# Moving the dense products of a three-layer gated graph network ahead in the order, and its last tiles ahead of them

## The chip, the cores and the metric

The kernel runs on one core of one Trainium2 chip. The metric is the device time of one execution in microseconds, as the median of several runs.

## What is computed

`x` has 12500 rows of 128 numbers, and there are 212500 edges `src -> dst`, sorted by `dst`. The reference normalises `x`, applies a ReLU and a linear layer, then runs three layers of message passing with a gated recurrent cell, and adds the result to `x`:

```python
h = jnp.maximum(_layernorm(x, axis=-1), 0.0)
h = h @ lin_w.T + lin_b
for i in range(3):
    m = h @ weight[i]
    agg = jax.ops.segment_sum(m[src], dst, num_segments=n_nodes)
    h = gru_cell(agg, h, w_ih, w_hh, b_ih, b_hh)
return x + h
```

A layer needs the messages `m` of all nodes of the layer before, since an edge may come from anywhere.

## The kernel before

Edges stand in 416 quads of 512 edges, and 28 quads make a superblock, of which there are 15. The sums `agg` are made in two ways. Of each superblock, 16 quads are **dense**: in the first part of layer one (the text counts layers from one, the code from zero) the kernel counts on the chip how often each source row feeds each destination, stores these counts as bytes, and from then on a dense quad's sum is a product of message rows and counts. The other 12 quads are **gathered**: POOL issues one indirect DMA for each 128 edges (line 600) into a ring of four steps' rows (`RING`), and PE adds them with one-hot matrices (line 880).

The program of each layer is a list of *steps*, the same for all engines. Step s of a layer handles two gathered quads: eight gathers on POOL, 24 matmuls on PE, two additions into `aggT` on DVE (line 1290). POOL may be four steps ahead of PE. Layer one has 144 steps, of which the last 46 (98 to 143) have dense work; layers two and three have 88 steps each. After a layer's last numbered step come a few more without gathers.

Dense work is counted in *units* of two or three blocks of 128 source rows; 42 units make one superblock's dense sum, 14 slices of three units. For one unit ACT widens the counts from bytes (`widen`, line 717), DVE splits the message rows into two halves (`split`, lines 1404 and 1406), and PE does two matmuls per block (`dense_block`, line 920). `wide_counts` and `message_halves` have two slices each (`UBUF`), so ACT and DVE can be six units ahead of PE. In every step with dense work PE takes `STEP_UNITS`, that is seven, units. When a superblock's 42 units are done, DVE adds its sum to `aggT` (line 1301).

A *tile* is 256 destination nodes, 49 of them. A tile's work begins in the first step after its quads have been added (`ready_after`, `schedule`): three products of the state (lines 838 to 840) and three of the sums (line 868) on PE, sigmoids on ACT (662, 665), then DVE and a tanh (672), the new state (1344). In the step after the next come the next layer's messages on PE (851), which ACT copies (690, 692) and which leave as three bf16 pieces in one store (706, `store`). In the last layer line 849 transposes the result and line 709 stores it. Where `gates_last` holds, a tile's products stand at the end of a step, after the units; otherwise ahead of them.

The layers join at one wait: POOL gathers nothing of layer n+1 until every message store of layer n has landed (`pool.wait_ge(s_mst, 16 * NT * layer)`, ahead of line 600). Up to 30 units of the next layer may be done ahead, because their message rows come from tiles that are long done (`dense_blocks(True)`, limited by `TAIL_SPARE`). The order on each engine is written out at build time by `layer_steps`; `dense_blocks` says which blocks belong to which step, `units_and_sums` puts a widen and a split six units ahead of their product.

## Time and profile before

| what | value |
|---|---|
| median of three runs | 3803.09 us (3802.09 to 3811.09) |
| the profiled execution's own time | 3803.88 us |
| its span, first to last instruction | 3802.1 us |
| busy share of the span | PE 88%, DVE 74%, ACT 80%, POOL 70% |
| chain that ended last, by engine | POOL 35%, PE 23%, issue 15%, ACT 15%, DVE 6%, DMA 4% |
| granted TensorE clock, mean | 0.96 of full speed |

The span has six stretches: the prologue and the counting up to about 1316 us; the dense steps of layer one, whose last gathered sum on PE begins at 1797.61 us; a passage in which the last tiles are finished, up to layer two's first gather at 1885.95 us; layer two, whose last gathered sum begins at 2812.16 us; a second passage, up to 2859.75 us; and layer three to the end. A view by stretches reads better here than the page's sums, because the engine that sets the pace changes. In a timeline row the columns are start in us, duration in us, engine, line, operation, output<-inputs, count, and in brackets the idle time ahead of the first instruction with what ended it. Rows of a timeline that follow each other on one engine and line are merged.

### The profile page before, as it was taken

To read this page: it belongs to the slowest core of one execution; us is meant where nothing else is said; L and a number is where in the kernel's file an instruction comes from. 1 tells how busy PE (TensorE), PEld (TensorE's weight loads), DVE (VectorE), ACT (ScalarE), POOL (GpSimd) and SP (SyncE) were. 2 spreads that over 40 slices of the span, in tenths; PEclk is the share of its full clock that TensorE was granted. 3 is DMA by queue.
4 is the path that set the end of the run, shared out by engine and by line. 5 is a ranking of instruction groups with operands and counts; after the bars stand their busy time and mean duration, and the time that the engine had idled before them with its cause. 6 is when DMAs were issued, how large, how long until landed. Compare 5 with 4: busy or idle time off the path is not lost.

```text
span 3802.1 us, 76920 instructions
## 1 busy us (share of the span) xinstructions
PE 3361.6 (88%) x24880; PEld 2652.7 (70%) x24881; DVE 2801.6 (74%) x7778; ACT 3044.4 (80%) x4427; POOL 2663.4 (70%) x2622
## 2 busy tenths in 40 slices
PE   5279888998999799999799999999987999999997
PEld 4156666666666577777577777777776877787775
DVE  7678787888887677777577777777775777777775
ACT  4268898888888788888788889888886888878784
POOL 4677776776766677775177777777736777777775
PEclk8589999999999899999899999999998999999999
DMA  8345545455554697776666777777775766666674
GB/s 273 112 120 191 175 156 181 148 184 166 164 184 145 194 275 213 212 212 187 196 199 201 219 207 217 218 207 214 210 226 180 207 203 202 205 201 205 200 210 126
DMA packets 445139, 736.12 MB, mean 194 GB/s; under 512 B 63688, under 2 KB 329032, under 8 KB 444744
## 3 DMA queue, kind: packets, MB, share of 16 engines
q1 hardware_dynamic: 206616, 402.21, 32.7%
q0 software_dynamic: 122880, 251.82, 24.5%
q10 hardware_dynamic: 115248, 77.10, 6.5%
q8 instruction: 213, 3.49, 0.4%
q14 instruction: 182, 1.49, 0.1%
HBM read 557.22 MB, written 173.67 MB: 192 GB/s over the span
## 4 chain that ended last, share of the span: by engine, by line
POOL 35%; PE 23%; issue 15%; ACT 15%; DVE 6%; DMA 4%; ACTq 1%; DVEq 0%; SPq 0%; POOLq 0%
POOL ring_region L600 34%; PE psum L903 16%; ACT wide_counts L717 10%; ACT half_counts L758 3%; DMA states<-temps 2%; DVE quad_onehots L1370 2%; PE psum L920 2%; PE psum L880 1%; PE psum L868 1%; DVE block_onehots L1354 1%; PE psum L811 1%; DVE temps L1330 1%; DMA messages_region<-counts 1%; PE psum L804 0%; ACTq L745 0%
## 5 line engine op out<-in xcount | busy, mean ns | idle before, releaser
L600 POOL DMA_INDIRECT ring_region<-messages,edge_src x2560 | 2609.2, 1019 | 1037.5 <-issue 764.2
L717 ACT CAST wide_counts<-messages_region 128x1024 fp32r<-128x1024 uint8 (+1 forms) x1596 | 1762.0, 1185 | 188.5 <-PE psum L920 155.1
L920 PE MATMUL psum<-wide_counts,message_halves 128*128 128x512 f32 x7448 | 1794.4, 398 | 70.3 <-DVE message_halves L1406 50.5
L920 PEld LDWEIGHTS psum<-wide_counts,message_halves 128*128 128x128 f32 x7448 | 1397.6, 191 | 374.8 <-ACT wide_counts L717 90.0
L903 PE MATMUL psum<-quad_onehots,block_onehots 128*128 128x266 bf16 (+1 forms) x6720 | 844.7, 272 | 104.2 <-ACT half_counts L758 63.8
L758 ACT CAST half_counts<-psum 128x490 f32 (+1 forms) x1680 | 846.9, 594 | 64.6 <-PE psum L903 40.2
L903 PEld LDWEIGHTS psum<-quad_onehots,block_onehots 128*128 128x128 bf16 x6720 | 576.4, 100 | 359.5 <-issue 137.0
L1406 DVE TENSOR_TENSOR message_halves<-messages_region,message_halves 128x256 fp32r<-128x256 f32 (+1 forms) x1596 | 751.0, 471 | 55.0
L1404 DVE CAST message_halves<-messages_region 128x256 fp32r<-128x256 f32 (+1 forms) x1596 | 611.4, 383 | 114.1 <-PE psum L920 75.7
L1370 DVE TENSOR_SCALAR quad_onehots<-iota_quad,count_keys 128x1176 bf16<-128x1176 f16 x960 | 560.7, 645 | 0.0
L880 PE MATMUL psum<-onehot,ring_region 128*128 128x36 bf16 x7680 | 245.0, 179 | 151.7 <-DMA ring_region<-messages,edge_src 140.8
L880 PEld LDWEIGHTS psum<-onehot,ring_region 128*128 128x128 bf16 x7680 | 230.8, 97 | 210.6 <-issue 180.0
L1354 DVE TENSOR_SCALAR block_onehots<-iota_block,count_keys 128x128 bf16<-128x128 bf16 x960 | 183.6, 271 | 137.9 <-PE psum L896 101.4
L1290 DVE TENSOR_TENSOR aggT<-aggT,psum 128x36 f32 x640 | 122.2, 191 | 216.4 <-PE psum L880 147.8
L1330 DVE SCALAR_TENSOR_TENSOR temps<-psum,small,temps 128x256 f32<-128x256 f32 x147 | 70.8, 482 | 241.3 <-ACT temps L662 236.4
L868 PE MATMUL psum<-aggT,wih 128*128 128x256 f32 x882 | 217.1, 383 | 3.7 <-DVE aggT L1301 3.7
L868 PEld LDWEIGHTS psum<-aggT,wih 128*128 128x128 f32 x882 | 169.8, 193 | 27.7 <-issue 4.1
L662 ACT ACTIVATE temps<-psum,small 128x256 f32<-128x256 f32 x147 | 69.0, 469 | 142.9 <-PE psum L868 142.7
L672 ACT ACTIVATE temps<-temps,small 128x256 f32<-128x256 f32 x147 | 76.2, 518 | 106.1 <-DVE temps L1332 105.9
L1265 DVE TENSOR_TENSOR onehot<-iota_block,edge_rel 128x288 bf16<-128x288 bf16 x320 | 144.7, 452 | 1.5 <-issue 1.5
L700 ACT CAST pieces_out<-temps 128x256 bf16<-128x256 f32 x98 | 41.9, 427 | 121.9 <-DVE temps L1309 121.9
L762 ACT CAST half_counts<-psum 128x98 f32 x210 | 128.1, 610 | 0.0
(132 smaller groups left out, 1788.4 us busy)
## 6 DMA issues: line engine op xcount, KB each, us to landing
messages_region<-counts SPq DMA_DIRECT2D x532, 462.0 KB
counts<-half_counts SPq DMA_DIRECT2D x210, 462.0 KB
ring_region<-messages,edge_src POOLq DMA_INDIRECT x2560
messages<-pieces_out ACTq DMA_DIRECT2D x98, 192.0 KB
messages_region<-plain SPq DMA_DIRECT2D x21, 896.0 KB, 8.0
temps<-states ACTq DMA_DIRECT2D x98, 128.0 KB
states<-temps ACTq DMA_DIRECT2D x98, 128.0 KB
plain<-temps ACTq DMA_DIRECT2D x98, 128.0 KB
```

Of the source, the lines that this page charges most:

```text
L600: nc.gpsimd.indirect_dma_start(out=rows[:, n % RING, h * QC + c, :], out_offset=None, in_=messages[layer], in_offset=bass.IndirectOffsetOn ...
L717: nc.scalar.copy(wide_counts[:, v % UBUF, here], stage[v % ABUF][:, here, :, 0:WW]).then_inc(s_wide, 1)
L758: nc.scalar.copy(half_counts[half][:, 2 * HB * i:2 * HB * (i + 1), own:WS][:, :, bass.ds(columns[j], W - own)], counted[:, 0:RW].rearrange ...
L868: nc.tensor.matmul(bank, wih[:, gate * P:(gate + 1) * P], nodes, start=alone, stop=True, skip_group_check=not alone).then_inc(s_gate, 1)
L880: mm = nc.tensor.matmul(window(n, h), rows[:, n % RING, i, k * P:(k + 1) * P], onehot[:, n % 3, i, :], start=(c == 0 and k == 0), stop=(c ...
L903: mm = nc.tensor.matmul(by_block[:, :, SUBLOW[c]:SUBLOW[c] + SUBW[c]], blocks_oh[j % 3][:, c, :], x_round, start=(k == 0), stop=True, skip ...
L920: mm = nc.tensor.matmul(psum[:, 6 + kg % 2, 0:2 * WW], halves[:, v % UBUF, b % HB, half * P:(half + 1) * P], wide_counts[:, v % UBUF, b % ...
L1265: nc.vector.tensor_tensor(onehot[:, n % 3, :, :], iota_lo[:, 0:W].unsqueeze(1).to_broadcast([P, 2 * QC, W]), edge_rel[:, first * QC:(first ...
L1354: made = nc.vector.tensor_scalar(blocks_oh[j % 3][:, c, :], iota_lo[:], los[:, col:col + 1], None, ALU.is_equal)
L1370: made = nc.vector.tensor_scalar(xs[j % 2][c], iota_x[:, 0:NB * SUBW[c]], keys[:, col:col + 1], -float(SUBLOW[c]), ALU.subtract, ALU.is_equal)
L1404: nc.vector.tensor_copy(high, whole).then_inc(s_high, 1)
L1406: nc.vector.tensor_tensor(low, whole, high.bitcast(F32), ALU.subtract).then_inc(s_low, 1)
```

## The change

Four things are altered. A step of layer one takes 7.5 units (7 and 8 in turn), a step of the other layers 7.25 (8 in every fourth). Tiles become due by the new pace, exactly counted, in place of a fixed lead of four steps. From the step before a layer's end on, a step has few units (3, then 3, 2 and the rest, `TAIL_UNITS`) and its tile comes first. And from the layer's end on a tile's store stands ahead of the step's widening on ACT.

```diff
-LEAD = 4
+TAIL_UNITS = (3, 3, 2, 20)
...
+    def units_to(layer, i):
+        return (2 * STEP_UNITS + 1) * i // 2 if layer == 0 else (4 * STEP_UNITS + 1) * i // 4
...
-        dense = begun + GSB - 1 - (LEAD if layer else 0)
+        lead = sum(TAIL_UNITS) if layer else 0
+        dense = DENSE_FROM[layer] + next(m for m in range(STEPS[layer])
+                                         if lead + units_to(layer, m + 1) >= UN * SLICES * (i + 1))
...
+        def step_units(layer, s):
+            if not ahead:
+                return STEP_UNITS
+            tail = (STEPS[layer] - 1, *(max(TILES_AT[layer]) + k for k in range(3)))
+            if layer < LAYERS - 1 and s >= tail[0]:
+                return TAIL_UNITS[tail.index(s)] if s in tail else TAIL_UNITS[0]
+            i = s - DENSE_FROM[layer]
+            return units_to(layer, i + 1) - units_to(layer, i)
...
-                now = end if whole else min(block_of(unit_of(d) + STEP_UNITS), max(d, end))
+                now = end if whole else min(block_of(unit_of(d) + step_units(layer, s)), max(d, end))
...
         def gates_last(layer, s):
-            return DENSE_FROM[layer] <= s < STEPS[layer]
+            return DENSE_FROM[layer] <= s < STEPS[layer] - 1
...
+                stores = [low_tile(layer, tiles_at, s, lag) for lag in (3, 2)
+                          if low_tile(layer, tiles_at, s, lag) is not None]
+                if s >= STEPS[layer]:
+                    for t in stores:
+                        store(layer, t)
                 for w in units.get((layer, s), ()):
                     widen(w)
-                for lag in (3, 2):
-                    if low_tile(layer, tiles_at, s, lag) is not None:
-                        store(layer, low_tile(layer, tiles_at, s, lag))
+                if s < STEPS[layer]:
+                    for t in stores:
+                        store(layer, t)
```

Worked out from the tables, the four last tiles and the units around them stand as follows; the number of units in all is the same, 366 up to the end of layer one, 600 for layer two with 30 of them done in layer one and 30 of layer three's done in layer two.

| | before | after |
|---|---|---|
| layer one: units before the sum of its last gathered step (143) | 315 | 337 |
| layer one: steps of its last four tiles | 146 to 149 | 143 to 146 |
| layer one: units after that sum, before the last store / behind it | 51 / 0 | 14 / 15 |
| layer two: units before the sum of its last gathered step (87) | 609 | 630 |
| layer two: steps of its last four tiles | 86, 87, 88, 89 | 84, 85, 86, 88 |
| layer two: units after that sum | 21 | 0 |
| layer three: steps of its last four tiles | 86, 87, 88, 89 | 84, 85, 86, 88 |

PE at the end of layer one, from the products of the last tile (48) to layer two's first gathered sum. 838 to 840 and 868 are a tile's products, 920 the dense matmuls, 851 the messages of the tiles 47 and 48, 880 the gathered sum; the changed file has all PE lines 20 higher. Before:

```order
L838 MATMUL psum<-temps,whh 128x256
L839 MATMUL psum<-temps,whh 128x256
L840 MATMUL psum<-temps,whh 128x256
L868 MATMUL psum<-aggT,wih 128x256 x3
L920 MATMUL psum<-wide_counts,message_halves 128x512 x32
L851 MATMUL psum<-wmsg,temps 128x128 x2
L920 MATMUL psum<-wide_counts,message_halves 128x512 x10
L851 MATMUL psum<-wmsg,temps 128x128 x2
L880 MATMUL psum<-onehot,ring_region 128x36 x24
```

With the change:

```order
L858 MATMUL psum<-temps,whh 128x256
L859 MATMUL psum<-temps,whh 128x256
L860 MATMUL psum<-temps,whh 128x256
L888 MATMUL psum<-aggT,wih 128x256 x3
L940 MATMUL psum<-wide_counts,message_halves 128x512 x14
L871 MATMUL psum<-wmsg,temps 128x128 x2
L940 MATMUL psum<-wide_counts,message_halves 128x512 x10
L871 MATMUL psum<-wmsg,temps 128x128 x2
L940 MATMUL psum<-wide_counts,message_halves 128x512 x70
L900 MATMUL psum<-onehot,ring_region 128x36 x24
```

Between the last tile's products and its messages there are 24 dense matmuls in place of 42, and 70, that is 15 units, now stand behind the messages.

ACT at the same place, from the last tile's tanh (672) on: 690, 692 and 700 are the copies of a tile's messages, 706 its store, 717 the widening; the changed file has these lines 15 higher. Before:

```order
L672 ACTIVATE temps<-temps,small 128x256
L674 ACTIVATE aggT<-ident 128x256
L687 DMA states<-temps 128x256
L690 COPY temps<-psum 128x256
L692 CAST pieces_out<-psum 128x2x128
L694 DMA plain<-temps 128x2x128
L700 CAST pieces_out<-temps 128x2x128
L717 CAST wide_counts<-messages_region 128x1024
L717 CAST wide_counts<-messages_region 128x1536
L706 DMA messages<-pieces_out 128x2x384
```

With the change:

```order
L687 ACTIVATE temps<-temps,small 128x256
L689 ACTIVATE aggT<-ident 128x256
L702 DMA states<-temps 128x256
L705 COPY temps<-psum 128x256
L707 CAST pieces_out<-psum 128x2x128
L709 DMA plain<-temps 128x2x128
L715 CAST pieces_out<-temps 128x2x128
L721 DMA messages<-pieces_out 128x2x384
L732 CAST wide_counts<-messages_region 128x1024
L732 CAST wide_counts<-messages_region 128x1536
```

The store of tile 47 leaves ahead of the two widenings of its step.

PE at the end of layer two, from its last gathered sum to layer three's first. Before, the first ten rows of it:

```order
L880 MATMUL psum<-onehot,ring_region 128x36 x24
L920 MATMUL psum<-wide_counts,message_halves 128x512 x32
L838 MATMUL psum<-third_state_tile,whh 128x256
L839 MATMUL psum<-third_state_tile,whh 128x256
L840 MATMUL psum<-third_state_tile,whh 128x256
L868 MATMUL psum<-aggT,wih 128x256 x3
L851 MATMUL psum<-wmsg,temps 128x128 x2
L838 MATMUL psum<-temps,whh 128x256
L839 MATMUL psum<-temps,whh 128x256
L840 MATMUL psum<-temps,whh 128x256
```

With the change, all of it:

```order
L900 MATMUL psum<-onehot,ring_region 128x36 x24
L871 MATMUL psum<-wmsg,temps 128x128 x4
L858 MATMUL psum<-temps,whh 128x256
L859 MATMUL psum<-temps,whh 128x256
L860 MATMUL psum<-temps,whh 128x256
L888 MATMUL psum<-aggT,wih 128x256 x3
L871 MATMUL psum<-wmsg,temps 128x128 x2
L900 MATMUL psum<-onehot,ring_region 128x36 x24
```

One tile and no unit is left behind the sum, where three tiles and 21 units stood.

## Rows read from the trace of the kernel before

**Rows 1.** POOL's gathers: grouped by line in layer two; the first nine alone (duration min/median/max).

```profile
L600 POOL DMA_INDIRECT ring_region<-messages,edge_src x704 | 703.2, 999 | 327.0 <-issue 213.9 <-DMA messages<-pieces_out 112.7 <-PE psum L880 0.3
...
L600 POOL DMA_INDIRECT ring_region<-messages,edge_src x9: 942/946/949, 1885.9 to 1895.9; - x9
```

**Rows 2.** Timeline of POOL: last gather of layers one and two, first of the next.

```profile
1772.18 1.03 POOL L600 DMA_INDIRECT ring_region<-messages,edge_src  x1 [0.30 <-issue]
...
1885.95 0.94 POOL L600 DMA_INDIRECT ring_region<-messages,edge_src  x1 [112.74 <-DMA messages<-pieces_out]
...
2802.32 1.03 POOL L600 DMA_INDIRECT ring_region<-messages,edge_src  x1 [0.30 <-issue]
2859.75 0.95 POOL L600 DMA_INDIRECT ring_region<-messages,edge_src  x1 [56.40 <-DMA messages<-pieces_out]
```

**Rows 3.** Groups of PE by line: layer two, 1898 to 2812; layer three, 2872 to 3776.

```profile
L920 PE MATMUL psum<-wide_counts,message_halves 128*128 128x512 f32 x2842 | 683.7, 397 | 26.9 <-DVE message_halves L1406 26.9
...
L880 PE MATMUL psum<-onehot,ring_region 128*128 128x36 bf16 x2075 | 66.2, 179 | 20.1 <-DMA ring_region<-messages,edge_src 20.0
...
L880 PE MATMUL psum<-onehot,ring_region 128*128 128x36 bf16 x2077 | 66.4, 179 | 54.9 <-DMA ring_region<-messages,edge_src 54.6
```

**Rows 4.** Timeline of PE, end of layer one: last gathered sum, last tile, next sum.

```profile
1797.61 0.76 PE L880 MATMUL psum<-onehot,ring_region 128*128 128x36 bf16 x24
...
1862.68 1.46 PE L868 MATMUL psum<-aggT,wih 128*128 128x256 f32 x6
...
1897.44 0.88 PE L880 MATMUL psum<-onehot,ring_region 128*128 128x36 bf16 x24 [17.65 <-DMA ring_region<-messages,edge_src]
```

**Rows 5.** Timeline of PE, end of layer two: last gathered sum, last tile, next sum.

```profile
2812.16 0.75 PE L880 MATMUL psum<-onehot,ring_region 128*128 128x36 bf16 x24 [2.02 <-DMA ring_region<-messages,edge_src]
...
2835.82 1.46 PE L868 MATMUL psum<-aggT,wih 128*128 128x256 f32 x6
...
2871.27 0.88 PE L880 MATMUL psum<-onehot,ring_region 128*128 128x36 bf16 x24 [17.87 <-DMA ring_region<-messages,edge_src]
```

**Rows 6.** The page's costliest groups: widening on ACT, the two halves on DVE.

```profile
L717 ACT CAST wide_counts<-messages_region 128x1024 fp32r<-128x1024 uint8 (+1 forms) x1596 | 1762.0, 1185 | 188.5 <-PE psum L920 155.1
...
L1406 DVE TENSOR_TENSOR message_halves<-messages_region,message_halves 128x256 fp32r<-128x256 f32 (+1 forms) x1596 | 751.0, 471 | 55.0
L1404 DVE CAST message_halves<-messages_region 128x256 fp32r<-128x256 f32 (+1 forms) x1596 | 611.4, 383 | 114.1 <-PE psum L920 75.7
```

**Rows 7.** Timeline of PE: gathered sums around a step with a tile and one without.

```profile
1764.99 0.77 PE L880 MATMUL psum<-onehot,ring_region 128*128 128x36 bf16 x24
...
1775.57 0.76 PE L880 MATMUL psum<-onehot,ring_region 128*128 128x36 bf16 x24
...
2790.30 0.77 PE L880 MATMUL psum<-onehot,ring_region 128*128 128x36 bf16 x24
...
2798.28 0.77 PE L880 MATMUL psum<-onehot,ring_region 128*128 128x36 bf16 x24
```

**Rows 8.** Timeline of ACT, end of layer one: a wait for a store, the last store.

```profile
1867.15 0.37 ACT L692 CAST pieces_out<-psum 128x256 bf16<-128x256 f32 x1 [2.60 <-DMA messages<-pieces_out]
...
1883.23 0.37 ACTq L706 DMA_DIRECT2D messages<-pieces_out  x1
```

**Rows 9.** Timelines of PE, end of layer three: last gathered sum, tiles 46, 47, 48.

```profile
3775.80 0.88 PE L880 MATMUL psum<-onehot,ring_region 128*128 128x36 bf16 x24 [7.80 <-DMA ring_region<-messages,edge_src]
3776.52 1.20 PE L838 MATMUL psum<-temps,whh 128*128 128x256 f32 x2
...
3782.29 0.67 PE L838 MATMUL psum<-temps,whh 128*128 128x256 f32 x2 [1.03 <-ACT temps L665]
...
3786.54 0.67 PE L838 MATMUL psum<-third_state_tile,whh 128*128 128x256 f32 x2 [1.21 <-ACT temps L665]
```

**Rows 10.** Timeline of ACT, end of layer two: a wait for a store, the last store.

```profile
2839.01 0.37 ACT L692 CAST pieces_out<-psum 128x256 bf16<-128x256 f32 x1 [2.11 <-DMA messages<-pieces_out]
...
2856.79 0.43 ACTq L706 DMA_DIRECT2D messages<-pieces_out  x1
```

More of the change, by code:

```diff
@@ L119, in gated_graph_layers @@
     STEP_UNITS = UN * SLICES // GSB
-    assert STEP_UNITS * GSB == UN * SLICES and STEP_UNITS <= UBUF * UN + 1
+    assert STEP_UNITS * GSB == UN * SLICES
+    def units_to(layer, i):
+        return (2 * STEP_UNITS + 1) * i // 2 if layer == 0 else (4 * STEP_UNITS + 1) * i // 4
     def block_of(unit):
```

## The prediction

> **What bounds the kernel now.** I read the busy shares first: PE is busiest, POOL least. They mislead, because the pace changes hands between stretches. So I went on to the groups of instructions by line inside each stretch, and then to the timelines of the two passages between layers.
>
> In layer two POOL waits for almost nothing: its gathers show 213.9 us of "issue", a fixed pause of some 0.30 us after each, and 0.3 us of waiting for PE [rows 1]. From the first gather of the layer, 1885.95, to the end of the last, 2802.32 + 1.03, it needs 917.4 us for 88 steps, 10.42 a step [rows 2]. PE meanwhile waits 20.0 us for rows in layer two and 54.6 in layer three [rows 3]. **Inside the layers two and three POOL sets the pace, and PE has a little room.** In layer one's dense part it is the other way: POOL's last gather starts at 1772.18, PE adds that step's rows only at 1797.61 [rows 2, 4]. There PE, fed by ACT and DVE, sets the pace.
>
> **The passages are the loss.** POOL stands idle for 112.74 us and for 56.40 us, each time until the last message store has landed [rows 2]. From the last gathered sum on PE to the next layer's first gather it takes 1885.95 - 1797.61 = 88.3 us, and 2859.75 - 2812.16 = 47.6 us [rows 2, 4, 5]. In them PE works on units of which seven stand around each of the last tiles; after the last store nothing is left for it, and it idles 17.65 and 17.87 us until the new rows come [rows 4, 5]. The change moves units out of the passages: in layer one ahead and behind, in layer two ahead only.
>
> **Prices.** A unit has 14/3 dense matmuls; 2842 of them keep PE busy 683.7 us [rows 3], so a unit costs PE 4.667 x 0.2406 = 1.12 us. ACT widens one in 1762.0 / 1596 = 1.10 us, and DVE splits one in 0.47 + 0.38 = 0.85 us [rows 6]. A step of seven units and a tile takes 1775.57 - 1764.99 = 10.58 us, one without a tile 2798.28 - 2790.30 = 7.98, so a tile costs PE 2.6 us [rows 7].
>
> **Term A, end of layer one.** 337 units instead of 315 now stand ahead of the last gathered sum: 22 x 1.12 = 24.7 us, and two tiles' messages more, 0.9. As PE sets the pace there, the sum comes 25.6 us later. Behind it: the sum and tile 45's products, 0.7 + 2.6 = 3.3 us. Then three more tiles, each with three units on PE: 3.4 + 2.6 = 6.0 us; ACT has three widenings (3.3) and a tile's seven short operations, so I take 6.5 and get 19.5. From tile 48's last product to the last store it is now 1883.23 - (1862.68 + 1.46) = 19.1 us [rows 4, 8]; nine widenings lie in it on ACT, five will, so 19.1 - 4 x 1.10 = 14.7. From the store to the first gather it is 2.7 us [rows 2, 8]. Together 40 in place of 88.3. Gain: 88.3 - 40 - 25.6 = **22.7 us**. The 15 units behind the store take PE 16.8 us. About 2.5 of that passes before the store leaves and 2.7 while it lands, so PE is ready some 12 to 13.5 us after the first gather, where the rows now need 1897.44 - 1885.95 = 11.5: the bubble is filled, at a cost of up to 2 us. Bounds: if the tail's cycles stay at 10.5 us, 12 less; if each of the 22 units costs what a unit costs with all of a step's waits (7 units in 10.58 us: 1.5), 8 less; the other way, tails as short as PE allows and no loss behind, 6 more.
>
> **Term B, layer two.** Now 973.8 us from its first gather to layer three's. PE has more to do before the last sum, 21 units and two tiles: 23.5 + 5.2 us. Against that stand 20.0 us of waiting for rows and 2.02 at the end [rows 3, 5], which go first. So the last sum comes 13.5 + (2812.16 - 1897.44) + 28.7 - 22 = 935 us after the first gather; some of the waits now are followed by slow matmuls, so I take 931. POOL alone would allow 917.4 + 1.8 = 919, PE without any of the room 957; these are the ends. Then the chain: the sum (0.7); tile 47's state, for which I take the 4.25 us from one tile to the next without units, 3782.29 to 3786.54 [rows 9]; tile 48's products, 2.6. From there to the last store it is now 2856.79 - (2835.82 + 1.46) = 19.5 us with seven widenings in it [rows 5, 10], without them 11.8; and 3.0 us to the gather. That makes 22 in place of 47.6. Layer two then takes 931 + 22 = 953: gain **20.8 us**. Nothing is left to fill this passage, but PE's idling there costs nothing that POOL does not cost anyway.
>
> **Term C, layer three.** PE has 54.6 us of room [rows 3] for 21 units ahead, so POOL's pace stands: the last sum comes, as now, 3775.80 - 2859.75 = 916 us after the first gather. Now 26.3 us follow with three tiles; then one. From tile 48's first product to the end it is 3802.1 - 3786.54 = 15.6; the sum ahead of it 0.7; and its matmuls will run at the slow rate of tile 46's (1.20 against 0.67 us for the first pair), some 1.7 us [rows 9]. Together 18: gain **8.3 us**.
>
> The earlier stores, `gates_last` and the tables cost nothing of their own: the same instructions in another order. SP's loads follow the widening, six units ahead as before.
>
> **Sum.** 22.7 + 20.8 + 8.3 = 51.8 us. The profiled execution took 3803.88 us (0.8 above the median of the runs shown), so I forecast **3752 us**, faster. A difference under 0.3%, 11.4 us, could hardly be told from none.
>
> **A rule that speaks against it.** POOL's gathers take 946 ns while DVE is idle, 999 on average in layer two [rows 1]: DVE's work stretches them by 0.4 us a step, seven units' worth. A quarter of a unit more adds 0.015 us a step, 2.6 us in two layers, which is within the sum's error. The Trainium skill, SBUF — State Buffer, section "Who interferes with whom", says that VectorE in its two-port modes (casts among them) and GpSimd hold their shared ports exclusively, the other being fully blocked. The trace agrees that there is stretching, but not that it is total. What such blocking in full would do here is the third rival.
>
> **Rivals.**
> 1. *The dense work does not hide.* The 22 and 21 units moved ahead cost 1.5 us each rather than 1.12, and PE's waits for rows stay, because they fall where POOL is ahead of a short step: 8 + 8 + 22 = 38 us back, 3790. For it: PE also waits 26.9 us for DVE's halves in layer two [rows 3]. Against: the waits for rows are PE being early. Chance 0.10.
> 2. *The tails stay slow.* A tile's copy on ACT waits until the store of the tile before has landed, 2.60 and 2.11 us [rows 8, 10]. If that, and not units, sets the tail's cycle, it stays near 10 us: 10.5 back in A and about 8 in B, 3771. Against: 4.25 us in layer three, though that has another store. Chance 0.12.
> 3. *The ports.* Each added cast stops a gather for its whole 0.38 us: 0.25 x 0.38 x 176 steps = 17 us, 3769. Against: 2.7 us of casts a step now lengthen a step's gathers by 0.4 us only. Chance 0.06.
> 4. *Steps of eight starve, and the kernel gets slower.* ACT and DVE can be six units ahead. If in a step of eight units the two that are not covered wait for DVE's whole pair, 2 x 0.85 = 1.7 us, then the 22 such steps of layer one lose 37 us, the 21 of layer two 36, the 20 of layer three 34, less the 26 us of room left there: 81 us, 3833. At 1.2 us in each of the 43 such steps of layers one and two nothing would be left of the gain, and from some 1.4 on it would show as slower. Against: steps of seven also exceed six, and PE's 26.9 us of such waits in layer two would be 0.3 a step. Chance 0.04.
>
> A better case, in which layer two's last sum follows POOL alone and the tails run as PE allows, gives 3752 - 12 - 6 - 4 = 3730; chance 0.05. That leaves 0.63 for the forecast.
>
> **Numbers.** The bounds of A (20 down, 6 up) and B (26 down, 12 up) do not all fall together; with rivals 2 and 3 and the better case inside, 3728 to 3787 should hold the time 8 times in 10. What is left out is rival 4, half of rival 1 and the tails of the others. Faster by over 0.3%: all but rival 4 and half of rival 1, 0.91; within 0.3%: 0.05; slower: 0.04.
>
> **What would show it.** In the profile after, POOL's idle times before the first gathers of layers two and three should fall from 113 to some 70 us and from 56 to some 35, and the passages from the last sum to the next layer's first gather should be near 40 us instead of 88 and near 22 instead of 48. PE's bubble before layer two's first sum should nearly vanish; before layer three's it should stay near 18. In layer two PE's waits for rows should shrink to a few us and its last sum come about 931 us after the first gather. Layer three should end some 18 us after its last sum. I am wrong if POOL starts to wait for PE inside the layers two and three, if PE's waits for halves multiply (rival 4), or if POOL's gathers get longer than 999 ns (rival 3).

## The result, and the profile after

The changed kernel takes **3761.65 us** (median; 3760.15 to 3772.1), the kernel before in the same comparison 3802.59. The ratio is 0.9895, with an interval of 0.9871 to 0.992; a second comparison later gave 0.9906 (0.989 to 0.9921). The forecast was 3752 us, faster, with a range of 3728 to 3787. Direction and range held. Of the three terms one came out as worked, one four fifths and one three fifths as large. One execution of all that follow, of the kernel of run 9, took 9389.65 us; no profile shows a reason, and that run's ratio leaves it out.

The stages, from the timelines of the two profiled executions (sum: the start of a step's gathered matmuls on PE; gather: the start of a layer's first gather on POOL):

| stage, us | before | after | forecast |
|---|---|---|---|
| layer one, the sum of step 99 to the last sum (143) | 454.0 | 483.0 | 25.6 more |
| passage one, last sum to layer two's first gather | 88.3 | 41.2 | 40 |
| layer two, first gather to last sum | 926.2 | 940.4 | 931 |
| passage two, last sum to layer three's first gather | 47.6 | 21.0 | 22 |
| layer three, first gather to last sum | 916.1 | 918.4 | 916 |
| from there to the end | 26.3 | 15.8 | 18 |
| span | 3802.1 | 3758.3 | |

The sum of step 99 is the first that stands behind dense work: step 98, the first dense one, has its sum ahead of its units. So 308 of the units lie in the first stage before the change and 330 after it.

POOL's timeline after, the last gather of layers one and two and the first of the next (columns as in [rows 2]):

```profile
1788.15 0.95 POOL L615 DMA_INDIRECT ring_region<-messages,edge_src  x1 [0.30 <-issue]
...
1862.73 0.94 POOL L615 DMA_INDIRECT ring_region<-messages,edge_src  x1 [73.63 <-DMA messages<-pieces_out]
...
2777.28 0.95 POOL L615 DMA_INDIRECT ring_region<-messages,edge_src  x1 [0.30 <-issue]
...
2824.09 0.95 POOL L615 DMA_INDIRECT ring_region<-messages,edge_src  x1 [45.86 <-DMA messages<-pieces_out]
```

POOL's idle times, 112.74 and 56.40 us [rows 2], are now 73.63 and 45.86. For the second I had said some 35. POOL itself is as quick as before in layer two, 2777.28 + 0.95 - 1862.73 = 915.5 us from first to last gather (before 917.4). What has grown is the time from there to PE's sum of that step: 2803.11 - 2778.23 = 24.9 us, against 2812.16 - 2803.35 = 8.8 before [rows 2, 5].

PE's timeline after, end of layer one: last gathered sum, the products of the tiles 46, 47 and 48, the units behind the last store, layer two's first sum [rows 4]:

```profile
1821.53 0.77 PE L900 MATMUL psum<-onehot,ring_region 128*128 128x36 bf16 x24
...
1830.23 0.60 PE L858 MATMUL psum<-temps,whh 128*128 128x256 f32 x2
...
1836.45 0.60 PE L858 MATMUL psum<-third_state_tile,whh 128*128 128x256 f32 x2
...
1842.70 0.60 PE L858 MATMUL psum<-temps,whh 128*128 128x256 f32 x2
...
1854.47 17.89 PE L940 MATMUL psum<-wide_counts,message_halves 128*128 128x512 f32 x70
1878.13 0.88 PE L900 MATMUL psum<-onehot,ring_region 128*128 128x36 bf16 x24 [5.77 <-DMA ring_region<-messages,edge_src]
```

A tile follows the other after 6.2 us; before, with seven units between them, such a step took 10.58 [rows 7]. The bubble of 17.65 us [rows 4] is 5.77. PE is not late in it: its 15 units end at 1872.36, 9.6 us after the first gather, and the rows come only 15.4 us after it, where they came after 11.5 before. SP's loads for further units run beside these gathers: three leave within 5 us of the first gather, among them this one of 896 KB, where before the change none left between 1.2 us ahead of the gather and the sum.

```profile
1864.57 0.38 SPq L551 DMA_DIRECT2D messages_region<-plain  x1
```

The profiles of all runs below bear this out. In the eleven first steps of layers two and three during which no load leaves, the rows are added 11.5 to 11.6 us after the first gather; in the eleven with loads in which PE waits for rows, after 12.9 to 16.0. That the loads are the cause fits, but no run changed them alone.

ACT at the same place [rows 8]:

```profile
1858.53 0.37 ACT L707 CAST pieces_out<-psum 128x256 bf16<-128x256 f32 x1 [0.40 <-DMA messages<-pieces_out]
...
1860.28 0.37 ACTq L721 DMA_DIRECT2D messages<-pieces_out  x1
1860.75 16.44 ACT L732 CAST wide_counts<-messages_region 128x1024 fp32r<-128x1024 uint8 x15 [0.95 <-PE psum L940]
```

The copy's wait for the store of the tile before, 2.60 us [rows 8], is 0.40, and the step's 15 widenings stand behind the last store, as the change orders them. Layer two starts 2.45 us after that store.

PE's timeline after, end of layer two: last sum, messages of tile 47, products and messages of tile 48, next sum [rows 5]:

```profile
2803.11 0.76 PE L900 MATMUL psum<-onehot,ring_region 128*128 128x36 bf16 x24
...
2808.23 1.20 PE L871 MATMUL psum<-wmsg,temps 128*128 128x128 f32 x4 [3.82 <-DVE temps L1329]
2809.22 1.06 PE L858 MATMUL psum<-temps,whh 128*128 128x256 f32 x2
...
2818.14 1.22 PE L871 MATMUL psum<-wmsg,temps 128*128 128x128 f32 x4 [3.68 <-DVE temps L1364]
...
2835.61 0.88 PE L900 MATMUL psum<-onehot,ring_region 128*128 128x36 bf16 x24 [16.25 <-DMA ring_region<-messages,edge_src]
```

PE's groups after: dense matmuls, the tiles' products and the gathered sums of layer two (1879 to 2803), then the sums of layer three (2836 to 3742) [rows 3]:

```profile
L940 PE MATMUL psum<-wide_counts,message_halves 128*128 128x512 f32 x2940 | 705.4, 396 | 29.7 <-DVE message_halves L1426 29.4
L888 PE MATMUL psum<-aggT,wih 128*128 128x256 f32 x288 | 70.0, 379 | 0.0
L900 PE MATMUL psum<-onehot,ring_region 128*128 128x36 bf16 x2065 | 66.3, 179 | 2.9 <-DMA ring_region<-messages,edge_src 2.9
...
L900 PE MATMUL psum<-onehot,ring_region 128*128 128x36 bf16 x2081 | 66.3, 179 | 48.8 <-DMA ring_region<-messages,edge_src 48.8
```

In layer two the waits for rows went from 20.0 (22.0 with the last sum's) to 2.9 us, and 98 dense matmuls more took 705.4 - 683.7 = 21.7 us. The waits for DVE's halves are 29.4 us (26.9 before). In layer three PE still has some 49 us of room. The view by stretches of layer two sums it up, first of the kernel before (1898 to 2812; us, busy time and count of PE, PEld, DVE, ACT, POOL, granted clock, DMA share, GB/s):

```profile
1898.00:2812.00 914.00, 865.12 (x5649) 710.96 (x5645) 677.62 (x1822) 780.37 (x926) 693.87 (x695) 0.99 0.72 213
```

The same of the changed kernel, and below it the tail of layer one, the passage at the end of layer two, and of this passage the part with tile 48's products:

```profile
1879.00:2803.00 924.00, 891.37 (x5765) 734.60 (x5765) 695.76 (x1878) 802.74 (x956) 688.90 (x691) 0.99 0.72 218
...
1823.00:1849.00 26.00, 24.06 (x115) 20.23 (x114) 19.52 (x51) 21.88 (x34) 0.00 (x0) 1.00 0.74 216
...
2804.00:2818.00 14.00, 6.63 (x20) 4.94 (x18) 6.36 (x17) 5.18 (x15) 0.00 (x0) 0.74 0.28 84
...
2809.00:2814.00 5.00, 5.00 (x14) 3.93 (x13) 0.42 (x1) 1.01 (x3) 0.00 (x0) 0.50 0.30 92
```

PE's busy time in layer two rose by 26.3 us, its idle time fell from 48.9 to 32.6, by 16.3.

POOL's gathers after, layer two, then layer one's dense part [rows 1]:

```profile
L615 POOL DMA_INDIRECT ring_region<-messages,edge_src x704 | 701.3, 996 | 287.8 <-issue 212.7 <-DMA messages<-pieces_out 73.6 <-PE psum L900 1.5
...
L615 POOL DMA_INDIRECT ring_region<-messages,edge_src x328 | 328.6, 1002 | 123.3 <-issue 95.1 <-PE psum L900 28.2
```

The end, on PE: last gathered sum, the first and last products of tile 48 [rows 9]:

```profile
3742.45 0.88 PE L900 MATMUL psum<-onehot,ring_region 128*128 128x36 bf16 x24 [6.13 <-DMA ring_region<-messages,edge_src]
...
3746.17 1.06 PE L858 MATMUL psum<-third_state_tile,whh 128*128 128x256 f32 x2
...
3748.73 1.84 PE L888 MATMUL psum<-aggT,wih 128*128 128x256 f32 x6
```

### The profile page after: what moved, and what is told of

It is laid out like the page before. It is cut to its first block, busy times and chain, and to the rows that moved or that the text cites. A ratio compares the mean times of both kernels' runs of the same rounds, so it can differ in the third digit from the quotient of the medians.

```text
span 3758.3 us, 76920 instructions
## 1 busy us (share of the span) xinstructions
PE 3358.3 (89%) x24880; PEld 2650.8 (71%) x24881; DVE 2798.8 (74%) x7778; ACT 3037.9 (81%) x4427; POOL 2655.0 (71%) x2622
## 3 DMA queue, kind: packets, MB, share of 16 engines
q0 software_dynamic: 122880, 251.82, 23.9%
## 4 chain that ended last, share of the span: by engine, by line
PE 33%; POOL 24%; ACT 17%; issue 12%; DVE 7%; DMA 5%; ACTq 1%; DVEq 0%; SPq 0%; POOLq 0%
POOL ring_region L615 24%; PE psum L923 16%; ACT wide_counts L732 12%; PE psum L940 9%; ACT half_counts L778 3%; DMA states<-temps 3%; DVE quad_onehots L1390 2%; PE psum L900 2%; PE psum L888 2%; DMA messages_region<-counts 1%; DVE temps L1350 1%; PE psum L871 1%; DVE temps L1352 1%; DVE block_onehots L1374 1%; PE psum L858 1%
## 5 line engine op out<-in xcount | busy, mean ns | idle before, releaser
L1424 DVE CAST message_halves<-messages_region 128x256 fp32r<-128x256 f32 (+1 forms) x1596 | 610.4, 382 | 86.1 <-PE psum L940 46.1
```

The source lines that it names most:

```text
L1424: nc.vector.tensor_copy(high, whole).then_inc(s_high, 1)
```

## The experiments

All are edits of the changed kernel. The theory was the prediction's: a unit costs PE its time where PE sets the pace, a unit ahead of the last store lengthens the passage, and behind the last store it fills a bubble. The stages of all of them, in us, from their profiles; the ratio is to the kernel before, with its interval:

| kernel | ratio | layer one, dense | passage one | layer two to last sum | passage two | layer three with its end |
|---|---|---|---|---|---|---|
| before | | 454.0 | 88.3 | 926.2 | 47.6 | 942.3 |
| the change | 0.9895 (0.9871 to 0.992) | 483.0 | 41.2 | 940.4 | 21.0 | 934.2 |
| the change again | 0.9906 (0.989 to 0.9921) | 482.2 | 42.4 | 939.3 | 18.6 | 933.9 |
| layer one alone | 0.9959 (0.9944 to 0.9974) | 487.1 | 41.0 | 926.8 | 47.6 | 941.8 |
| layers two and three alone | 0.9945 (0.9929 to 0.9962) | 457.4 | 86.1 | 942.0 | 22.3 | 933.9 |
| stores late | 0.993 (0.9908 to 0.9953) | 483.5 | 55.5 | 942.7 | 19.5 | 936.1 |
| sevens in layer one's tail | 0.9956 (0.9942 to 0.9969) | 485.3 | 61.2 | 941.9 | 19.7 | 932.5 |
| pace seven | 0.9929 (0.991 to 0.9949) | 484.3 | 41.6 | 929.0 | 35.5 | 944.3 |
| 15 kept back | 0.9856 (0.9831 to 0.9881) | 487.7 | 42.7 | 922.8 | 25.7 | 934.2 |
| 15 kept back, spaced | 0.9872 (0.9854 to 0.989) | 483.6 | 41.7 | 925.2 | 22.6 | 934.1 |
| 21 kept back | 0.985 (0.9829 to 0.9872) | 487.7 | 42.7 | 917.8 | 21.3 | 933.5 |
| 21 kept back again | 0.9866 (0.9846 to 0.9886) | 484.2 | 42.5 | 921.9 | 21.7 | 935.8 |
| lean in both layers | 0.9855 (0.9839 to 0.987) | 481.9 | 36.7 | 924.8 | 19.3 | 936.8 |

Where a stage has the same units in several runs, it differs among them by up to 6 us in layer one's dense part and by 1 to 4 us elsewhere. Differences of that size are not read as effects below.

**1. Layer one alone.** The layers two and three, their tiles, tails and stores as before the change.

```diff
-        return (2 * STEP_UNITS + 1) * i // 2 if layer == 0 else (4 * STEP_UNITS + 1) * i // 4
+        return (2 * STEP_UNITS + 1) * i // 2 if layer == 0 else STEP_UNITS * i
...
-            if not ahead:
+            if not ahead or layer:
...
-            return DENSE_FROM[layer] <= s < STEPS[layer] - 1
+            return DENSE_FROM[layer] <= s < STEPS[layer] - (layer == 0)
```

> Layer one's part of the change alone: 7.5 units a step there, its sparse tail, its early stores; layers two and three as before (seven units a step, tiles by the fixed lead, stores behind the widening). If the terms stand each for itself: the dense steps of layer one some 29 us longer, the passage to layer two's first gather 41 us in place of 88, layer two and three as in the kernel before, 974 and 942 us; in all some 18 us faster than before, about 3785 us. Rival: the 15 units pushed behind the last store only shift PE's work into layer two, where PE has 20 us of room that is needed elsewhere; then layer two is 10 us or more longer than 974 and the time is near 3795 us.

Measured: ratio 0.9959. Passage one fell as in the change, from 88.3 to 41.0 us, and layer two took what it took before, 926.8 us to its last sum. So the 15 units behind layer one's last store cost layer two nothing there. In time it is 14.3 us, where I expected 18.

**2. Layers two and three alone.** Layer one as before.

```diff
-        return (2 * STEP_UNITS + 1) * i // 2 if layer == 0 else (4 * STEP_UNITS + 1) * i // 4
+        return STEP_UNITS * i if layer == 0 else (4 * STEP_UNITS + 1) * i // 4
...
-            if not ahead:
+            if not ahead or layer == 0:
...
-            return DENSE_FROM[layer] <= s < STEPS[layer] - 1
+            return DENSE_FROM[layer] <= s < STEPS[layer] - (layer > 0)
```

> The part of layers two and three alone: 7.25 units a step there and tiles due by that pace; layer one as before. If the terms stand each for itself: layer one's passage 88 us, layer two about 960 us in place of 974 with a passage of 21 us at its end, layer three 934 in place of 942; some 21 us faster than before, about 3782 us. Rival: layer two's longer way to its last sum (940 us in the changed kernel, 926 before) comes from the 15 units that layer one pushes into its beginning, not from its own pace; then the last sum comes 926 to 930 us after the first gather here, and the time is near 3772 us.

Measured: ratio 0.9945. The two parts add up: 0.41% and 0.55% against the change's 1.05 and 0.94%. And with layer one as before, layer two's last sum still comes 942.0 us after its first gather. What was missing from term B is made in layer two itself, by its own 21 units, and not handed on from layer one.

**3. Stores late.** The tiles' stores stand behind the step's widening everywhere, as before the change.

```diff
-                if s >= STEPS[layer]:
+                if False:
                     for t in stores:
...
-                if s < STEPS[layer]:
+                if True:
```

> The changed kernel with each tile's store behind the step's widening again, all else kept. If the store's landing is on the chain of the sparse tail: each store leaves three widenings, 3.3 us, later, the next tile's copy waits for it, and layer one's passage grows from 41 to 45 to 50 us; layer two's passage has no widenings and stays at 21; in all 4 to 8 us slower than the changed kernel. Rival: units on PE set the tail's cycle, the stores are not on the chain: the passage stays at 41 to 42 us and the time at 3761 us.

Measured: ratio 0.993, and passage one 55.5 us, 14.3 longer; I had expected less. I had overlooked that the last store's own step is the one with the 15 units. ACT's timeline of this kernel, the widenings and the last store:

```profile
1859.20 11.80 ACT L732 CAST wide_counts<-messages_region 128x1024 fp32r<-128x1024 uint8 x11
1870.86 0.37 ACTq L721 DMA_DIRECT2D messages<-pieces_out  x1
```

Eleven widenings, 11.8 us, run before the store leaves. It leaves 11.2 us later after the last sum than in the change, and lands 5.5 us after that instead of 2.45. Passage two, without units, is as in the change. So it is the earlier stores that keep these units' widenings behind the last store.

**4. Sevens in layer one's tail.** Seven units after each of the last four tiles (eight after the last), none behind the last store.

```diff
-TAIL_UNITS = (3, 3, 2, 20)
+TAIL_UNITS = (7, 7, 7, 20)
...
-        lead = sum(TAIL_UNITS) if layer else 0
+        lead = 4 * STEP_UNITS if layer else 0
```

> The change, but in layer one seven units instead of three follow each of the tiles 45 to 48, so that all 29 units of the tail stand ahead of the last message store and none behind it. The earlier stores stay. Theory (what shortens the passage is the number of units ahead of the last store): 15 more units x 1.10 to 1.12 us, so the passage from layer one's last gathered sum to the next gather goes from 41.2 to 57 to 58 us, PE idles some 9 to 11 us again before layer two's first sum, which then comes 11.5 us after the gather instead of 15.4; as PE sets layer two's pace, those 3.9 us come back there. The time is 12 to 17 us above the change's. Rival (the tail's cycle is set by a tile's stores and copies, not by units): the tile's cycle stays near 6.2 us, the passage at 41 to 45 us, the time within 5 us of the change's.

Measured: ratio 0.9956; passage one 61.2 us, 20 more than the change for 15 units, and the time 19 to 23 us above the change's, where I expected 12 to 17. PE's timeline of this kernel, the products of the tiles 46 to 48, the last tile's messages, layer two's first sum:

```profile
1841.67 0.60 PE L858 MATMUL psum<-temps,whh 128*128 128x256 f32 x2
...
1852.43 0.60 PE L858 MATMUL psum<-third_state_tile,whh 128*128 128x256 f32 x2
...
1862.78 0.60 PE L858 MATMUL psum<-temps,whh 128*128 128x256 f32 x2
...
1881.11 1.20 PE L871 MATMUL psum<-wmsg,temps 128*128 128x128 f32 x4 [5.63 <-DVE temps L1329]
1899.89 0.88 PE L900 MATMUL psum<-onehot,ring_region 128*128 128x36 bf16 x24 [17.59 <-DMA ring_region<-messages,edge_src]
```

The cycle is 10.4 to 10.8 us again instead of 6.2. Units set it, and the rival (a tile's own stores and copies) falls. The bubble is back in full, 17.59 us; I had expected 9 to 11. One part of the theory failed: PE now starts layer two 11.5 us after the first gather instead of 15.4, yet the last sum comes no earlier (941.9 against 940.4). **Here a start 4 us later at the layer's head cost nothing at its end.** The distance of PE's sum behind the end of the same step's gathers shows why: 5.6 us in the change and 1.8 here at the first step, 3.2 and 4.3 five steps later. PE makes it up at once; begun earlier, it waits for rows instead, 7.4 us in the layer against 2.9.

**5. Pace seven.** The layers two and three at 7.0 units a step as before, but with the sparse tail.

```diff
-        return (2 * STEP_UNITS + 1) * i // 2 if layer == 0 else (4 * STEP_UNITS + 1) * i // 4
+        return (2 * STEP_UNITS + 1) * i // 2 if layer == 0 else STEP_UNITS * i
```

> The change, but the layers two and three advance by 7.0 units a step, as before the change; layer two's tail is sparse all the same: tiles 45 to 48 at the steps 86 to 89, with 7, 3, 3, 3 and 2 units around them and 10 behind the last store. It asks what the 7.25 units a step are worth when the tail is sparse in any case. Theory (in layer two a unit ahead of the last sum costs its PE time, so the pace only moves work): last sum of layer two 918 to 926 us after its first gather (the change: 940.4), but two more tiles and their units behind it, so that passage is 33 to 40 us instead of 21; layer two together 955 to 963 us against 961.4. Layer three ends with two or three tiles behind its last sum again, tail 20 to 25 us against 15.8. Time from 3 below to 8 above the change's. Rival (the pace is what brings the gain): layer two is as long as before, 970 us or more, and the time 15 us or more above the change's.

Measured: ratio 0.9929, 9 to 13 us over the change (0.9906 and 0.9895). Of these, 10 are in layer three (944.3), which has its tiles behind the last sum again, where I had allowed for 4 to 9; layer two as a whole takes 929.0 + 35.5 = 964.5 us against 961.4. It is neither theory's time. The pace is worth its 10 us in layer three, where PE has room, and in layer two next to nothing: what it takes from the passage it adds ahead of the last sum.

**6. 15 units kept back.** Layer two ends like layer one: 14 units in its last steps, 15 behind the last store.

```diff
+            if 0 < layer < LAYERS - 1 and s >= STEPS[layer] - 5:
+                return (3, 4, 4, 3, 0, 0, 0, 20)[s - STEPS[layer] + 5]
```

(with the rule for `TAIL_UNITS` left to layer one)

> The changed kernel, but in layer two the last 15 of the 30 units done ahead stay behind the last store, as in layer one: steps 83 to 86 take 3, 4, 4, 3 units in place of 8, 7, 7, 7, and 15 follow the last tile. Theory: PE, not POOL, sets layer two's last sum in the changed kernel, by the units ahead of it; 15 x 1.12 = 17 us less bring that sum from 940 to 924 us after the first gather (POOL's own floor is 917), the passage stays at 21 us, PE's bubble before layer three's first sum falls from 16 us to under 5, and layer three, which POOL paces, keeps 934 us: some 15 us faster than the changed kernel, about 3746 us. Rival: PE's lateness is made of waits spread over the layer, not of units that could stand elsewhere, or layer three pays for the 15 units: under 5 us faster.

Measured: ratio 0.9856. The last sum comes 922.8 us after the first gather instead of 940.4, so PE's arrears were indeed the cause. From gather to gather layer two takes 948.5 us instead of 961.4. Passage two grew by 4.7 us, which I had not foreseen, and all of it lies ahead of tile 47's messages, which come 10.2 us after the last sum instead of 5.1. With three or four units between them the last tiles follow each other after 7 to 8 us. DVE's new state of tile 46 waits for a state store to land, and what stands behind it on DVE and ACT, tile 47's state among it, comes later. DVE's timeline of this kernel, tile 46's new state:

```profile
2798.04 0.43 DVE L1366 TENSOR_TENSOR temps<-temps 128x256 f32<-128x256 f32 x1 [3.72 <-DMA states<-temps]
```

PE's timeline, the messages of tile 47:

```profile
2807.30 1.19 PE L873 MATMUL psum<-wmsg,temps 128*128 128x128 f32 x4 [7.67 <-DVE temps L1331]
```

**7. The same, spaced.** The 14 units as 2, 3, 3, 6, so that six stand between the tiles 46 and 47.

```diff
-                return (3, 4, 4, 3, 0, 0, 0, 20)[s - STEPS[layer] + 5]
+                return (2, 3, 3, 6, 0, 0, 0, 20)[s - STEPS[layer] + 5]
```

> The earlier variant with 15 of layer two's units kept for the time behind its last store, with the same 14 units in the steps 83 to 86 spread as 2, 3, 3, 6 instead of 3, 4, 4, 3, so that six units instead of three stand between the tiles 46 and 47. Theory (the passage there was 25.7 instead of 21 us because tile 47's state had to wait for the state store of a tile only 7 us ahead): last sum of layer two as there, 922 to 924 us after the first gather, passage 20 to 22.5, layer two 943 to 946 against 948.5; time 2 to 5 us below that variant. Rival (the passage is longer because the units that stood between the last tiles had hidden something else, or because of the 15 behind): passage 24.5 to 27, no difference.

Measured: passage two 22.6 us, 3 shorter, but the last sum 2.4 us later, and the ratio 0.9872: no difference in time. Tile 47's messages come 7.2 us after the last sum instead of 10.2, so the 3 us are gained where run 6 lost them, though a wait for a state store is still there. DVE's timeline, tile 47's new state:

```profile
2804.23 0.43 DVE L1366 TENSOR_TENSOR temps<-temps 128x256 f32<-128x256 f32 x1 [2.99 <-DMA states<-temps]
```

PE's timeline, the messages of tile 47:

```profile
2805.14 1.20 PE L873 MATMUL psum<-wmsg,temps 128*128 128x128 f32 x4 [5.93 <-DVE temps L1331]
```

Both differences, 3.1 and 2.4 us, are of the size of the spread given above; that the spacing makes either of them is not shown.

**8. 21 units kept back.** Now 609 units stand ahead of layer two's last sum, as many as before the change.

```diff
-                return (3, 4, 4, 3, 0, 0, 0, 20)[s - STEPS[layer] + 5]
+                return (0, 1, 2, 5, 0, 0, 0, 25)[s - STEPS[layer] + 5]
```

> The same with six units more kept back: 0, 1, 2, 5 in the steps 83 to 86, 21 behind layer two's last store. Theory (with 15 kept back POOL's pace is nearly reached, and beyond it nothing is to be had): last sum 917 to 920 us after the first gather, passage 21 to 24, PE ready only some 21 us after layer three's first gather instead of 16, which that layer's room of 55 us takes up without loss; time within 4 us of the run with the spread 2, 3, 3, 6. Rival (PE still sets the pace in layer two, each unit kept back gives its 1.1 to 1.3 us): last sum 915 or less, time 6 to 8 us below. Rival (a late PE at the head of layer three is not made up): g-to-sum of layer three 5 us longer than 918 to 919, time above.

Measured: ratio 0.985. POOL's last gather of layer two in this kernel and the next layer's first:

```profile
2778.07 0.94 POOL L617 DMA_INDIRECT ring_region<-messages,edge_src  x1 [0.30 <-issue]
2805.12 0.94 POOL L617 DMA_INDIRECT ring_region<-messages,edge_src  x1 [26.11 <-DMA messages<-pieces_out]
```

PE's last sum of layer two, the units behind the last store, layer three's first sum:

```profile
2783.82 0.85 PE L902 MATMUL psum<-onehot,ring_region 128*128 128x36 bf16 x24 [2.57 <-DMA ring_region<-messages,edge_src]
...
2800.57 24.08 PE L942 MATMUL psum<-wide_counts,message_halves 128*128 128x512 f32 x98
2824.49 0.77 PE L902 MATMUL psum<-onehot,ring_region 128*128 128x36 bf16 x24
```

The sum comes 4.8 us behind POOL's last gather and has waited for rows: POOL's pace is reached, at 917.8 us. POOL's idle time is 26.11 us. PE begins layer three 19.4 us after the first gather, and layer three takes 933.5 us as in the change, so that late start too is free. The time is 9.5 us below run 7's, where I had allowed 4; the repeat in run 9 stands only some 2 us below run 7 by its ratio, so most of the rest is the spread of runs.

**9. The change again, and 21 kept back again**, side by side on one chip.

> The change itself once more, so that the variants of the same call stand beside it on one chip: 0.987 to 0.992 of the kernel before.

> The variant with 21 units behind layer two's last store once more. If its advantage is real, its interval lies wholly below that of the change: 0.983 to 0.987, 15 to 22 us less than the change, all of it in layer two (939 against 961 us from gather to gather).

Measured: 0.9906 (0.989 to 0.9921) and 0.9866 (0.9846 to 0.9886). The intervals do not meet. From gather to gather layer two takes 943.5 us against 958.0; the difference is about 14.5 us or 0.4%.

**10. Lean in both layers.** In layer one's tail one unit after each tile, 24 behind the last store, and layer two as in run 8 (the tiles' lead stays at 28 units).

```diff
-TAIL_UNITS = (3, 3, 2, 20)
+TAIL_UNITS = (1, 1, 1, 26)
```

> The variant with 21 units behind layer two's last store, and in layer one's tail one unit instead of three after each tile, 24 instead of 15 behind the last store. Theory (a unit behind the last store is free as long as PE makes up its late start within the layer, and the run with the sevens showed a start 4 us earlier to be worth nothing at the layer's end): the tail's cycle falls from 6.2 to 5 to 5.5 us, passage one from 42 to 31 to 36 us; PE starts layer two 23 to 26 us after its first gather instead of 15.4, is level with POOL again within 20 steps, and layer two stays at 937 to 942 us. Time 5 to 11 us below the run with 21 behind. Rival (the late start is not made up, since PE has hardly any room in layer two): layer two is 6 to 10 us longer, POOL waits for PE at its head, the time within 3 us of that run. Rival (the tile's own chain of copies and stores sets a tail as lean as that): passage one stays at 39 to 42 us.

Measured: 0.9855 (0.9839 to 0.987) beside 0.9866 for run 8 in the same comparison: the fastest median of that comparison, 3745.85 against 3751.09 us, but not separable. Passage one is 36.7 us, just above the expected 31 to 36, and layer two 944.1 as in run 8's repeat. PE starts layer two only 16.3 us after the first gather, not 23 to 26: much of the 24 units is done before. The passage would be shorter still, had the last store not landed later. ACT's timeline of this kernel, the last store:

```profile
1857.12 0.37 ACTq L723 DMA_DIRECT2D messages<-pieces_out  x1
```

POOL's timeline, the first gather of layer two:

```profile
1863.13 1.03 POOL L617 DMA_INDIRECT ring_region<-messages,edge_src  x1 [68.94 <-DMA messages<-pieces_out]
```

From store to gather it is 6.0 us, in the change 2.45. SP's timelines of the two kernels show what stands ahead: here the load of the next message rows (896 KB) leaves 1.5 us before the store, in the change 9 us before it. SP in this kernel:

```profile
1855.63 0.38 SPq L553 DMA_DIRECT2D messages_region<-plain  x1
```

SP in the change:

```profile
1851.26 0.38 SPq L551 DMA_DIRECT2D messages_region<-plain  x1
```

That the load delays the store fits these rows. In run 3 such a load leaves 1.3 us before the last store, which takes 5.5 us; in the 24 other passages of the thirteen profiles no such load leaves in the 7 us before the last store, and it takes 2.2 to 3.0. A run with the load moved was not made.

## Why the prediction was right, and where its sizes were off

**Which engine sets the pace where** was right for layer one, where PE's additions cost their full price, and for layer three. For layer two, "POOL sets the pace, and PE has a little room" held for the kernel before; the change used the room up. From step 20 of the layer on PE falls behind: 3.5 us behind the gathers at step 20, 15.5 at step 40, 22.0 at step 80, 24.9 at the last. In the steps 20 to 39, in which 13 tiles fall, PE is busy for 211 us, while POOL needs 208 for its gathers; in the first 20, with 9 tiles, for 199. POOL hardly notices, since the ring is four steps deep (it waits 1.5 us for PE), but what PE owes at the last step stands on the path in full.

**Term B** was mis-sized, 12.4 us in place of 20.8 (973.8 - 961.4), and the step that failed is "some of the waits now are followed by slow matmuls, so I take 931". Summed as it stood, the working gave 935. Of it, PE's added work was priced a little high, 28.7 us for the 26.3 measured, but only 16.3 us of idle time went where I took 22: 19.1 us of waits for rows went, and 2.5 of waits for halves came. From sum to sum that is 10.3 us instead of 6.7. The other 2 us is PE's start, 15.4 us after the gather where I put 13.5. It is set by the late rows and not by PE's units; by run 4 an earlier start would have gone into waits for rows. The discount of 4 us had no row behind it. The passage, 22 forecast, was 21.0. Runs 6 and 8 confirm the cause: with fewer units ahead of the last sum it comes at 922.8 and at 917.8, next to POOL's own 919.

**Term A** gave 88.34 - 41.20 - 28.99 = 18.2 us in place of 22.7. The passage was right within 1.2 us, and in its parts: 23.9 us from the last sum to tile 48's last product (22.8 taken), 14.8 from there to the last store (14.7), 2.45 to the gather (2.7). The term that came out larger is the 22 units moved ahead, with two tiles' messages: 29.0 us where 25.6 was forecast. In the profiled pair the dense matmuls took 372.2 - 343.4 = 28.8 us more instead of 24.7. The 102 matmuls more account for some 24.4 of it. The rest is that each one took 241.5 ns of PE's time where it took 238.6, at a granted clock of 0.99 of full speed instead of 1.00. Run 2, with the old number of units in layer one, has 240.9 ns at 0.98, so the slower matmuls come without the added units too. Over all profiles this stretch takes 454 to 457 us with 308 units and 482 to 488 with 330, on average 28.9 us more, some 1.3 a unit. How much of the excess is the clock's and how much the units' stays open. The value lies inside the bounds I had set (1.5 us a unit).

What the prediction had wrong in this term cost no time: it has PE ready 12 to 13.5 us after layer two's first gather, the rows after 11.5 and the bubble filled. PE was ready after 9.6, since its units began 5.8 us ahead of the store and not 2.5, the rows came after 15.4, and a bubble of 5.77 us was left.

**Term C** was right: 942.3 - 934.2 = 8.1 us, forecast 8.3. The last sum stayed at POOL's pace and the end fell to 15.8 us.

**"The earlier stores cost nothing of their own"** is right as a price and misleads as a reading: without them run 3 loses 14.3 us, because they carry the 15 units behind the last store.

**The sum**: 18.2 + 12.4 + 8.1 = 38.7 us, against 51.8. The spans differ by 43.8; the other 5.1 lie ahead of layer one's dense part, which the change does not touch and which began that much earlier in the profiled execution. By the ratios the change is worth 36 to 40 us.

**The rivals.** 1 (the units cost 1.5 each and the waits for rows stay) fell on the waits, 2.9 us, and was half right on the price, with some 1.3 a unit in layer one. 2 (the tails stay slow) was refuted by the 0.40 us wait and by run 4. 3 (the ports): gathers last 996 ns on average in layer two, 999 before. The Trainium skill, SBUF — State Buffer, section "Who interferes with whom", describes exclusive holding of the shared ports; nothing here shows a quarter of a unit more per step to cost a gather anything. 4 (steps of eight starve): PE's waits for halves are 18.4 us in layer one's dense part, where before they were 20.6, and 29.4 in layer two, so eight units are fed as well as seven. The sign that POOL "starts to wait for PE" was named for the layers two and three; in layer two it is 1.5 us. In layer one POOL does wait for PE, 28.2 us, which costs nothing there, as PE sets the pace.

## What to carry to other kernels

Where one engine may run steps ahead of another through a ring, look at how far the second lags at the last step before a barrier, not at whether the first ever waits: that lag is paid in full. A late start after the barrier was free here, 4 us in layer two and 8 us (19.4 us after the first gather instead of 11.5) in layer three, because the second engine had room in the steps that follow. Work that fills time should stand behind the last thing a barrier waits for, and neither among the last tiles nor ahead of the last sum; that version (run 8) gained about 1.4% where the change gained 1.0. When such work is moved, check what it pushes ahead of the barrier's last store on every queue, widenings on the same engine as well as loads.

## What the runs showed of the hardware

A store of 192 KB landed, by the wait that it ended, 2.2 to 3.0 us after its issue in 24 passages between layers. It took 5.5 and 6.0 us in the two where a load of 896 KB had left 1.3 and 1.5 us ahead of it. The rows of a layer's first step were added 11.5 to 11.6 us after the first gather in the eleven cases in which no load left beside the gathers, and after 12.9 to 16.0 in the eleven in which loads did and PE waited for the rows. In the passage at the end of layer two PE waited 3.82 us and then worked on tile 48's products; from 2809 to 2814 us the granted clock was 0.50 of full speed, the lower of its two levels, and a pair of these products took 1.06 us. In the tail of layer one, with three units between the tiles and PE busy for 24.1 of 26 us, it was 1.00 and the pair took 0.60.
